# Attention scores by seven half-size products, outputs added in DRAM

## The reference

```python
h = group_norm(x, gn_w, gn_b)                 # 32 groups, eps 1e-5
q, k, v = split(qkv_w @ h + qkv_b)            # 512 x 1024 each
attn = softmax(q.T @ k / sqrt(512), axis=-1)  # 1024 x 1024
o = attn @ v.T                                # 1024 x 512
out = x + out_w @ o.T + out_b
```

## Time and profile before

| what | value |
|---|---|
| median of 3 runs | 2134.47 us (2133.47 to 2136.08) |
| the profiled execution's own time | 2135.79 us |
| its span | 2132.8 us |
| TensorE busy | 2118.6 us, 9340 matmuls |
| VectorE busy | 1382.1 us |
| ScalarE busy | 801.5 us |
| GpSimd busy | 275.2 us |
| granted TensorE clock, mean | 0.999 |

### The profile page before, as it was taken

The page is one execution under the profiler, slowest core; times in us unless marked ns, Lnnn a source line. Parts: engine busy times, 40 slices in busy tenths (PEclk is TensorE's granted clock), DMA queues, the critical chain, the costliest instruction groups (busy, mean ns, idle before and its releaser), DMA issues.

```text
span 2132.8 us, 23156 instructions
## 1 busy us (share of the span) xinstructions
PE 2118.6 (99%) x9340; PEld 1752.8 (82%) x9340; DVE 1382.1 (65%) x1885; ACT 801.5 (38%) x1179; POOL 275.2 (13%) x109
## 2 busy tenths in 40 slices
PE   8999999999999999999999999999999999999999
PEld 6788888888888888888888888888888888888887
DVE  6683766848567485675847758476683866748555
ACT  6441614426143351533515244162442614326141
POOL 2020111101111011110111102011020111101110
PEclk9999999999999999999999999999999999999999
DMA  5101020010201101010010200102001020110001
GB/s 165 41 21 60 2 79 2 30 50 2 79 2 35 46 10 70 2 56 25 16 65 2 79 2 21 60 2 79 2 30 50 2 79 2 35 45 6 35 1 40
DMA packets 48635, 76.16 MB, mean 36 GB/s; under 512 B 20400, under 2 KB 21136, under 8 KB 48528
## 3 DMA queue, kind: packets, MB, share of 16 engines
q1 hardware_dynamic: 47664, 72.32, 9.8%
q0 software_dynamic: 864, 2.36, 0.6%
HBM read 38.32 MB, written 33.98 MB: 34 GB/s over the span
## 4 chain that ended last, share of the span: by engine, by line
PE 97%; POOL 0%; DVE 0%; issue 0%; DVEq 0%; POOLq 0%
PE ring L194 32%; PE ring L196 32%; PE ring L195 32%; POOL xs L484 0%; DVE tv_lo L640 0%; DVE xs L590 0%; DVE key_raw L593 0%; DVE xs L702 0%; DVE ring L696 0%; POOL bqk L498 0%; DVE keybias L595 0%; DVEq L695 0%; POOLq L142 0%
## 5 line engine op out<-in xcount | busy, mean ns | idle before, releaser
L194 PE MATMUL ring<-h_hi,tv_hi 128*128 128x512 f32 x1024 | 399.2, 390 | 1.9 <-DVE tv_lo L640 1.9
L196 PE MATMUL ring<-h_hi,tv_lo 128*128 128x512 f32 x1024 | 399.0, 390 | 0.0
L195 PE MATMUL ring<-h_lo,tv_hi 128*128 128x512 f32 x1024 | 398.9, 390 | 0.0
L194 PE MATMUL ring<-p_hi,tv_hi 128*128 128x512 f32 x1024 | 398.3, 389 | 0.0
L195 PE MATMUL ring<-p_lo,tv_hi 128*128 128x512 f32 x1024 | 398.3, 389 | 0.0
L196 PE MATMUL ring<-p_hi,tv_lo 128*128 128x512 f32 x1024 | 398.3, 389 | 0.0
L419 ACT ACTIVATE tv_hi<-ring,t_bias 128x512 fp32r<-128x512 f32 x128 | 88.3, 690 | 660.3 <-PE ring L196 660.3
L398 ACT ACTIVATE stage<-ring,keybias 128x512 f32<-128x512 f32 x256 | 173.5, 684 | 275.3 <-PE ring L196 266.0
L403 ACT ACTIVATE stage<-stage 128x512 f32<-128x512 f32 x256 | 161.6, 631 | 209.3 <-DVE stage L661 209.3
L194 PEld LDWEIGHTS ring<-h_hi,tv_hi 128*128 128x128 f32 x1024 | 192.6, 188 | 41.9 <-DVE tv_lo L640 1.9
L640 DVE SCALAR_TENSOR_TENSOR tv_lo<-ring,t_bias,tv_hi 128x512 fp32r<-128x512 f32 x128 | 95.4, 750 | 201.3 <-ACT tv_hi L419 196.7
(11 more groups left out here) (103 smaller groups left out, 2910.7 us busy)
## 6 DMA issues: line engine op xcount, KB each, us to landing
xs<-x_in SPq DMA_DIRECT2D x64, 512.0 KB, 5.9
out<-xs SPq DMA_DIRECT2D x128, 256.0 KB, 2.0
xs<-xs POOLq DMA_DIRECT2D x3, 512.0 KB, 8.3
xs<-wk SPq DMA_DIRECT2D x4, 256.0 KB, 3.8
xs<-wq SPq DMA_DIRECT2D x4, 256.0 KB, 5.0
stage<-wv SPq DMA_DIRECT2D x4, 256.0 KB, 8.0
stage<-wo_t SPq DMA_DIRECT2D x4, 256.0 KB, 9.1
stage<-stage POOLq DMA_DIRECT2D x3, 256.0 KB, 3.4
```

Of the source, the lines that this page charges most:

```text
L194: nc.tensor.matmul(ps_out, st_hi, m_hi, start=first, stop=False)
L195: nc.tensor.matmul(ps_out, st_hi, m_lo, start=False, stop=False)
L196: return nc.tensor.matmul(ps_out, st_lo, m_hi, start=False, stop=last)
```

## The change

The 1024 by 1024 scores are taken as two by two blocks of 512, and their eight block products are replaced by seven (Strassen's scheme in Winograd's form). Four sums of blocks of h (`t1` to `t4`) and four of blocks of t (S1 to S4) are formed on VectorE and split into high part and rest like all operands. A product has 4 tiles of 6 matmuls. A11, S2, S3 and A22 (the products are named by their t side) accumulate in banks 0 to 3 one after the other, and the state between two of them is copied out; A12, S1 and S4 go to banks 4 to 7 and are added by VectorE to what was copied.

The ring is replaced by fixed banks, so output unit j and the next image's t unit j use bank j. `stage` has 16 tiles. `subtract_max`, the exponential, `p_part` and `p_rest` take two tiles (1024 columns) at a time. There is one input buffer: after the scores' first product ScalarE adds the output bias to x in place, SP stores it to the output, waits, and loads the next image; VectorE scales each output tile into one of three buffers, and GpSimd adds it to DRAM by an accumulating transfer. The sums are inverted after a trip through DRAM that spreads them over partitions, and so is the key bias.

```diff
-            def score_units(b, nb):
-                here = slice(nb * HALF, (nb + 1) * HALF)
-                for m in range(MT):
...
+            def score_products(b):
+                for p, (a, name) in enumerate(PRODUCTS):
+                    own_bank = p in (P_A12, P_S1, P_S4)
+                    for i in range(CT):
+                        cs = slice(i * P, (i + 1) * P)
+                        if i == 0:
+                            pe.wait_ge(s_tlo, b * 14 + 2 * a + 2)
+                            if name[0] == "t":
+                                pe.wait_ge(s_hplo, b * 4 + int(name[1]))
+                        if p in (P_A11, P_A12):
+                            t_bank_read(b, 4 * own_bank + i)
+                        elif p == P_S1:
+                            pe.wait_ge(s_c11, b * 4 + i + 1)
+                        elif p == P_S2:
+                            pe.wait_ge(s_p1, b * 4 + i + 1)
+                        elif p == P_S3:
+                            pe.wait_ge(s_p2, b * 4 + i + 1)
+                        elif p == P_A22:
+                            pe.wait_ge(s_p3, b * 4 + i + 1)
+                        else:
+                            pe.wait_ge(s_c22, b * 4 + i + 1)
+                        at = ring[:, 4 * own_bank + i, :]
+                        opens = p in (P_A11, P_A12, P_S1)
+                        for kk in range(2):
+                            m = three(at, t_part(r_hi, a, kk)[:, cs], t_part(r_lo, a, kk)[:, cs],
+                                      moving(h_hi, r_hi, name, kk), moving(h_lo, r_lo, name, kk),
+                                      opens and kk == 0, kk == 1, not opens)
+                        m.then_inc(s_unit, 1)
```

The banks of t in the first image are one place on (`t_bank`), and the order of its units is changed:

```diff
+T_ORDER = [(0, 1), (1, 1), (2, 1), (3, 1), (0, 0), (1, 0), (2, 0), (3, 0)]
+        def t_bank(b, j):
+            return (j + 1) % 8 if b == 0 else j
+            def t_bank_read(b, bank):
+
+                j = [t_bank(b, j) for j in range(8)].index(bank)
+                if j < 2:
+                    pe.wait_ge(s_a21, b * 2 + j + 1)
+                else:
+                    pe.wait_ge(s_tsum, b * 8 + (1, 2, 4, 6, 7, 8)[j - 2])
```

ScalarE's order behind the scores:

```diff
+                exponential(b, 0, 0)
+                p_part(b, 0, 0)
+                exponential(b, 0, 1)
+                v_hi_part(b, 0)
+                p_part(b, 0, 1)
+                exponential(b, 0, 2)
+                v_hi_part(b, 1)
+                p_part(b, 0, 2)
+                exponential(b, 0, 3)
+                v_hi_part(b, 2)
+                p_part(b, 0, 3)
+                v_hi_part(b, 3)
+                v_hi_part(b, 4)
+                v_hi_part(b, 5)
+                exponential(b, 1, 0)
+                p_part(b, 1, 0)
+                v_hi_part(b, 6)
+                v_hi_part(b, 7)
+                for q in range(1, CT):
+                    exponential(b, 1, q)
+                    p_part(b, 1, q)
```

VectorE's order for an image, from the t stage to the end of the sums:

```diff
+                for kk in range(2):
+                    t_direct_rest(b, A22, kk)
+                    t_sum(b, S1, kk)
+                if b > 0:
+                    scale_output(b - 1, 1, 3)
+                for kk in range(2):
+                    t_sum_rest(b, S1, kk)
+                for kk in range(2):
+                    t_direct_rest(b, A11, kk)
+                    t_sum(b, S2, kk)
+                    t_sum(b, S3, kk)
+                for a in (S2, S3):
+                    for kk in range(2):
+                        t_sum_rest(b, a, kk)
+                key_bias(b)
+                for kk in range(2):
+                    t_direct_rest(b, A12, kk)
+                    t_sum(b, S4, kk)
+                for kk in range(2):
+                    t_sum_rest(b, S4, kk)
+
+                for i in range(CT):
+                    add_scores(b, P_A12, i, i, s_p1, s_c11)
+                    if i > 0:
+                        max_step(b, 0, i, i, s_c11, b * 4 + i + 1)
                 if more:
...
+                    for q in range(CT * NB):
+                        stats_part(b + 1, q)
+                for i in range(CT):
+                    add_scores(b, P_S1, i, 12 + i, s_p3, s_c22)
+                    if i > 0:
+                        max_step(b, 1, i, CT + i, s_c22, b * 4 + i + 1)
+                for i in range(CT):
+                    max_step(b, 0, CT + i, CT + i, s_c21, b * 4 + i + 1)
+                for i in range(CT):
+                    add_scores(b, P_S4, i, 8 + i, s_p2, s_c12)
+                    max_step(b, 1, CT + i, i, s_c12, b * 4 + i + 1)
+
+                if more:
+                    group_variance(b + 1)
+                subtract_max(b, 0, 0)
+                subtract_max(b, 0, 1)
                 v_rest(b, 0)
+                p_rest(b, 0, 0)
+                subtract_max(b, 0, 2)
                 v_rest(b, 1)
...
+                p_rest(b, 0, 1)
+                subtract_max(b, 0, 3)
+                v_rest(b, 2)
+                p_rest(b, 0, 2)
+                v_rest(b, 3)
+                p_rest(b, 0, 3)
+                v_rest(b, 4)
+                if more:
+                    group_spread(b + 1)
+                sum_tree(b, 0)
+                v_rest(b, 5)
+                subtract_max(b, 1, 0)
+                subtract_max(b, 1, 1)
+                v_rest(b, 6)
+                v_rest(b, 7)
```

The input's way and the outputs':

```diff
+                for k in range(CT):
+                    sp.wait_ge(s_shifted, b * CT + k + 1)
+                    sp.dma_start(out_v[b, :, k, :], xs[:, k, :]).then_inc(s_sent[k], DMA)
                 if b + 1 < B:
+                    for k in range(CT):
+                        sp.wait_ge(s_sent[k], (b + 1) * DMA)
+                        sp.dma_start(xs[:, k, :], x_v[b + 1, :, k, :]).then_inc(s_x[k], DMA)
                     group_stats(b + 1)
...
+            def add_output(b, nb, c):
+                n = b * 8 + nb * CT + c
+                here = slice(nb * HALF, (nb + 1) * HALF)
+                if nb == 0:
+                    pool.wait_ge(s_sent[c], (b + 1) * DMA)
+                pool.wait_ge(s_scaled, n + 1)
+                nc.gpsimd.dma_start(out_v[b, :, c, here], scaled[n % 3][:, :],
+                                    accum_op=ALU.add).then_inc(s_added[n % 3], DMA)
```

More of the change, by code:

```diff
@@ L178, in _ @@
                     group_stats(b + 1)
[L179 to L187 removed]
+                own_sums(b, 0)
@@ L188, in _ @@
+                spread_inverses(b, 0)
+                own_sums(b, 1)
+                spread_inverses(b, 1)
+                if b + 1 < B:
+                    key_bias(b + 1)
             for k in range(CT):
-                sp.wait_ge(s_stored[k], B * NB * DMA)
+                sp.wait_ge(s_sent[k], B * DMA)
+            for y in range(3):
+                sp.wait_ge(s_added[y], (B * 8 - y + 2) // 3 * DMA)
         @block.tensor
         def _(pe):
[L193 to L213, removed]
+            def three(ps_out, st_hi, st_lo, m_hi, m_lo, first, last, goes_on=False):
+                nc.tensor.matmul(ps_out, st_hi, m_hi, start=first, stop=False, skip_group_check=goes_on)
+                nc.tensor.matmul(ps_out, st_hi, m_lo, start=False, stop=False, skip_group_check=goes_on)
+                return nc.tensor.matmul(ps_out, st_lo, m_hi, start=False, stop=last, skip_group_check=goes_on)
@@ L220, in weight_vector, with product_step @@
                 a.then_inc(s_vec, 1)
[L222 to L230, removed]
+            def product_step(w, k, banks, between=None):
                 pe.wait_ge(s_wlo[w], k + 1)
@@ new lines, in max_step @@
+            def max_step(b, nb, step, m, ready, count):
+                dve.wait_ge(ready, count)
+                first = stage[:, (0, 12)[nb], :]
+                if step == 1 and b > 0:
+                    dve.wait_ge(s_added[nb], (b * 8 - nb + 2) // 3 * DMA)
+                if step > 1:
+                    dve.wait_ge(s_rmax[nb], b * 7 + step - 1)
+                    first = run_max[nb][:, :]
+                nc.vector.tensor_tensor(run_max[nb][:, :], first, stage[:, 8 * nb + m, :], ALU.max).then_inc(s_rmax[nb], 1)
@@ L740, in _ @@
-                for m in range(1, MT):
-                    max_step(b, 0, m)
-                    if more and m < MT - 1:
-                        stats_part(b + 1, m - 1)
-                if more:
-                    stats_part(b + 1, 6)
-                    stats_part(b + 1, 7)
-                for m in range(MT):
-                    subtract_max(b, 0, m)
-                    if m >= 2:
-                        sum_step(b, m - 1)
-                    if m >= 1:
-                        p_rest(b, 0, m - 1)
-                    if m >= 4:
-                        max_step(b, 1, m - 3)
-                    if more and m == 5:
-                        group_variance(b + 1)
@@ L787, in _ @@
-                inverse(b, 1)
-                for c in range(CT if not more else CT - 1):
-                    scale_output(b, 1, c)
-                    add_input(b, 1, c)
+                p_rest(b, 0, 1)
[8 more added lines that the diff above has]
+                sum_tree(b, 0)
```

(12 more changed lines are left out.)

647 lines of the change are left out of this document (368 added, 279 removed).

## The result

The changed kernel takes 2241.95 us (median of 4 runs, 2240.99 to 2242.57) against 2134.89 us beside it: ratio 1.0501, 95% interval 1.0483 to 1.052. It is 5.0% slower. The forecast was 2190 us, slower, with 2225 as the upper end. The direction and the place of the wait were right; the loss forecast, about 55 us, was half of the 107 us measured.

A forecast was written before the change was run, and what follows sets the result against it. TensorE, busy 99% of the span, bounds the kernel. 2135.8 - 87.0 (matmuls) + 105.4 (wait) + 22.4 (clock) + 12 (start) + 2.5 (end) = 2191.1, put at 2190 us for the median; range 2115 to 2225, own range 2165 to 2212.

The forecast's parts named there:

- the place of the wait: Output stage's first unit: TensorE waits for v's seventh rest, 6.67 us in each image, 5.3 in the last.
- The removed matmuls: Scores stage: 168 matmuls instead of 192, saving 5.44 us an image, 87.0 us over 16 images.
- What is hidden: t stage, product tiles, x's trip, output banks, spread sums and key bias: all cost nothing.
- The chain to v's seventh rest: VectorE and ScalarE steps from S4's end at 59.84 release TensorE at 92.35 us instead of 85.68.
- v's fifth, the group's copies: 80.97: VectorE ahead of the sum tree: v rest five 0.60 us, the group's copies 0.16, done at 80.97.
- The collision: Second half's first subtraction, beside GpSimd's reduction of sums, ends with it at 88.8; without it the wait would be 5.0.
- The clock: TensorE behind each pause: a granted clock of 0.50 costs 1.4 us an image, 22.4 in all.
- The upper end given, 2.8: Slow clock behind TensorE's pause: upper end is twice the 1.4 us an image, lower end 0.
- Start and end: First image's scores begin later, taken as 12 us; the last store by GpSimd's queue adds 2.5 us.
- long case: First image: key dot reduction holds the first rest, first product at about 73, 13.5 us later; 8.5 if not held.
- Rival C: VectorE's round runs about 5 us ahead, so no wait on v's seventh rest: 2062 us, faster; chance 0.14.
- Rival D: Second wait at next t stage or x's trip, or slow clock twice as long: 2212 to 2250 us; chance 0.13.

The follow-up runs named there:

- early power: Changed kernel with GpSimd's power moved between the two maximum reductions instead of behind the second: 2197.83 us, ratio 1.0292.
- no power: Changed kernel with the power of images 2 to 16 left out, VectorE writing variance + 2 eps in its place: 2204.26 us, ratio 1.0327.
- v_first: Changed kernel with VectorE taking v's rests 5 to 7 right behind rest 4, and ScalarE v's high parts first: 2063.87 us, ratio 0.9666.
- spread_late: Changed kernel with VectorE's copies that wait for GpSimd's power moved behind the last v rest: 2174.64 us, ratio 1.0184.
- v_first_start: v_first with the first image's rests of h's sums ahead of the key dot products: 2060.17 us, ratio 0.9651.
- v_first_start2: v_first_start with S4's steps also ahead of the rests of S2 and S3 in the first image: 2059.84 us, ratio 0.965.

## Why the prediction was right in kind and short in size

- **The removed matmuls**: right, 168 in 38.08 us; 87 us.
- **What is hidden**: right. Shifting x began at 28.0 us of the image (28.1), its statistics were done at 43.6 (45.8), the t and product stages have no idle time.
- **The chain to v's seventh rest**: right to within 0.3 us up to the start of the fifth rest. The step that failed is "v's fifth, the group's copies: 80.97". The copies were given 0.16 us and no wait. GpSimd's power was taken to follow the second maximum at once; it follows after 7.04 us, and VectorE stood at the head of the chain for 3.77. In the 14 full images this wait was 3.9 us in the mean. The kernel before has the same pause, 7.1 us in the mean, as its view of waits shows. There nothing urgent stood behind it, and I did not carry it over.

```profile
POOL group_rstd L506 <- issue: 106.7, 15, 7.7
```

- **The collision**: the mechanism was right, its time wrong for the same reason. The pause ahead of the sums' reduction moved it to a later subtraction, where it costs nothing, and took off 1.8 us (4.15 less 2.35). This pause too lay in the rows of before: the next step behind the tree starts at 1183.83, the reduction of its sums only at 1189.96. The runs with the early power and with no power bring it back and show the forecast's 92.3 us (the last steps of the forecast chain add up to 92.28, not to the 92.35 written there).
- **Net**: 3.9 less 1.8 is 2.1 us more: a delay of 8.8 us (mean of 14 images, 8.4 to 9.3) in place of 6.67, some 32 us in all. In the last image, which has no group steps, TensorE came 5.3 us late (2191.03 for an image from 2100.01), as forecast, with the collision.
- **The clock**: the term of 1.4 us an image was too small. In the 14 images it measured 2.4 to 2.8 us; the means are an image of 136.5, less 125.12 and 8.8, so 2.6, about 19 us more in all. The upper end given, 2.8, holds it.
- **Start and end**: first product at 73.39, 13.7 us behind the kernel before. The forecast's long case, in which the rests are held, gave about 73; its sum took 12, so it was 1.7 short. From the end of the last matmul to the end of the span it is 5.9 us against 4.1, so 1.8 of the forecast 2.5.

2190 + 32 + 19 + 1.7 - 0.7 = 2242, against 2241.95.

The Trainium skill, "SBUF — State Buffer", Who interferes with whom, calls the port pair that VectorE shares with GpSimd an exclusive lock, says of VectorE's two-port modes that it is held for the whole instruction, and of two SBUF inputs only that they contend with GpSimd's reads; the prediction took these together. Read so, it would have moved the early-power run's subtraction to start at 1207.02 + 3.24 = 1210.26; two of them, 2.35 us, would then have ended at 1212.6. They ended at 1207.33 + 4.15 = 1211.48. The row decides, as it did ahead of the result.

Rival C (no wait, 2062 us) did not describe this kernel; its condition and nearly its number are those of `v_first`. Rival D, 2212 to 2250, is nearest in number, in part by luck: it named a clock slow for twice as long, which nearly came (2.6 against 1.4 us), but not the wait for the power; the second waits that it did name, on the next t stage and on x, did not arise.

## What to carry to other kernels

When work is cut from the busiest engine, write down by when it wants each of its inputs, and look at what stands ahead of those steps in the written order of the others; here a sum of 4 us and two small copies with a wait of 4 us ahead of them, none of which anybody wanted yet, with two steps of ScalarE and two subtractions, turned a gain of 3.3% into a loss of 5.0%. Take over every pause that the trace of before has, those too that cost nothing there, above all those put down to nothing but "issue". A wait inside an in-order queue is priced by what stands behind it.

## What the hardware did that was not expected

- GpSimd pauses 6.6 to 7.8 us when it goes from a cross-partition reduction to the power, and 5.8 to 6.6 us on the way back, counted from the end of the sums that it waits for or, where that was later, of the power. With the power left out there is no such pause between reductions. The Trainium skill, "GPSIMD Engine Reference", 2.1 Instruction dispatch, gives about 6 us without an instruction of its own in the profile for the first call of a freshly loaded GpSimd kernel. The way back agrees with it, the way to the power is about 1 us longer. That the pause returns in every image is what these runs show; that it is a loading of code is not shown by them. The way back runs during a wait in one case and after it in another. In the early-power run the maximum's reduction started 0.14 us after its subtraction, its wait being its own. The sums' reduction, whose wait is a separate instruction ahead of it (`lone_wait`), paid the 6.2 us after the wait. That the place of the wait makes the difference fits both but was not tried by itself.
- The clock's price varies for the same pauses. In the `spread_late` run two images with pauses of 0.65 and 3.56 us, and 0.63 and 3.56, had 12 and 5 matmuls at half speed behind them, 2.8 and 1.5 us. In the first image, behind the `out_bias` pause, the granted clock was 1.00 in `v_first_start` (1.99 us, 54.80 to 58.00) and 0.55 in `v_first_start2` (1.98 us, 54.40 to 58.20). What sets that was not looked into.
- A VectorE subtraction with two SBUF inputs against GpSimd's reduction of 512 columns ended with it, as in the earlier trace rows: in the early-power run the reduction ended at 1210.26, and ScalarE's exponential, which follows the subtraction, began at 1210.38. The reduction itself took 3.24 us there and up to 4.29 us in the changed kernel, and 6.95 to 7.52 us in each of the first 15 images of the `spread_late` run. What sets that was not looked into.
